# A four-stage token kernel on one Trainium2 core: the modulation row spread by DMA instead of by matmuls, the output accumulated by halves, the attention penalties gathered by type

## The reference, cut to what matters

```
# layer 0, per sequence: 16 decaying sums over time of the same gated input
gated  = x * sigmoid([x, ema(x)] @ Wg + bg)
mod    = 0.5 + sigmoid(gelu(x @ Wn1 + bn1) @ Wn2 + bn2)        # (256 tokens, 16)
traces = [causal_ema(gated * mod[:, d:d+1], tau_raws[d]) for d in range(16)]
temporal = sum_d traces[d] * softmax(blend)[d]
out = layernorm((gelu(x @ Wsoma) * sigmoid(temporal @ Wtemp)) @ Wout)
# layer 1, attention pooling: the score depends on the key alone, the mask on the type 0, 1 or 2
score[j, l] = v . tanh(W1 x[l] + b1)  -1e30 where l > j (type 0), l < j (type 1) or l == j (type 2)
# layer 2: 8 experts and a shared one, F = 1024, each scaled by a gate of the sequence
x += sum_e coef[e] * (silu(x @ Wg[e]) * (x @ Wu[e])) @ Wd[e]
# layer 3: a head with 192 shared output columns and 64 that are chosen per sequence
x += gelu(x @ W1 + b1) @ [W2, We[index]] + bias
```

## Time and profile before

| | |
|---|---|
| Runs shown | 2933.64, 2936.31 and 2940.9 us; median 2936.31 us |
| Profiled execution | 2936.55 us, of which the span from first to last instruction is 2934.7 us |
| Mean granted clock of PE | 0.986 of 2.4 GHz |
| Busy | PE 97%, PEld 81%, DVE 62%, ACT 49%, POOL 41% |
| Chain that ended last | PE 88%, DVE 7%, issue 2%, ACT 2% |
| DMA | 185.87 MB, on average 63 GB/s; share of the 16 engines' span 20% |

### The profile page before, as it was taken

How to read it: one execution, slowest core, us unless ns; L and a number is a source line. 1 busy time by engine, 2 the same in 40 slices (tenths; PEclk the granted TensorE clock), 3 DMA queues, 4 the chain that set the end, 5 groups by cost and what they waited for, 6 DMA issues and landing times.

```text
span 2934.7 us, 37380 instructions
## 1 busy us (share of the span) xinstructions
PE 2837.9 (97%) x13486; PEld 2373.1 (81%) x13486; DVE 1809.2 (62%) x2922; ACT 1433.5 (49%) x2466; POOL 1195.4 (41%) x931
## 2 busy tenths in 40 slices
PE   4799999999999999999999999999999999999998
PEld 3588888878888887887888888888888888888887
DVE  7669777776665586656665567566555556333443
ACT  1244663475345563456434555356533446334544
POOL 4216336524543345423454235532444433333333
PEclk7899999999999999999999999999999999999999
DMA  2222231121111121113111112111211112111331
GB/s 102 84 94 91 81 101 59 55 74 58 51 49 47 45 83 61 45 40 99 44 44 44 47 41 89 44 44 57 70 49 49 49 49 91 57 43 49 119 97 38
DMA packets 75688, 185.87 MB, mean 63 GB/s; under 512 B 8936, under 2 KB 21744, under 8 KB 75504
## 3 DMA queue, kind: packets, MB, share of 16 engines
q1 hardware_dynamic: 73648, 179.17, 19.5%
q0 software_dynamic: 1280, 4.20, 0.5%
q10 hardware_dynamic: 576, 0.11, 0.0%
HBM read 179.25 MB, written 4.19 MB: 63 GB/s over the span
## 4 chain that ended last, share of the span: by engine, by line
PE 88%; DVE 7%; issue 2%; ACT 2%; DMA 0%; POOL 0%; DVEq 0%; SPq 0%; ACTq 0%
PE bank L512 19%; PE bank L514 19%; PE bank L513 19%; PE ps_out L512 9%; PE ps_out L514 9%; PE ps_out L513 9%; PE bank L505 3%; DVE w_lo L1080 2%; DVE trace L994 2%; DVE trace L1002 1%; PE bank L582 1%; PE ps_out L667 1%; DVE hid L1109 0%; DVE acc L1126 0%; DVE trace L1060 0%
## 5 line engine op out<-in xcount | busy, mean ns | idle before, releaser
L1233 POOL TENSOR_TENSOR hid_lo<-hid,hid_hi 128x512 fp32r<-128x512 f32 (+1 forms) x640 | 849.1, 1327 | 1559.2 <-ACT hid_hi L886 1559.0
L512 PE MATMUL bank<-res_lo,w_hi 128*128 128x512 f32 (+1 forms) x2432 | 948.9, 390 | 4.7 <-issue 3.9
L514 PE MATMUL bank<-res_hi,w_hi 128*128 128x512 f32 (+1 forms) x2432 | 937.7, 386 | 0.0
L513 PE MATMUL bank<-res_hi,w_lo 128*128 128x512 f32 (+1 forms) x2432 | 936.9, 385 | 0.0
L1109 DVE TENSOR_TENSOR hid<-hid,bank 128x512 f32<-128x512 f32 (+1 forms) x608 | 399.1, 656 | 636.2 <-PE bank L514 526.5
L876 ACT ACTIVATE hid<-bank 128x512 f32<-128x512 f32 (+1 forms) x608 | 349.7, 575 | 728.5 <-PE bank L514 652.9
L1080 DVE TENSOR_TENSOR w_lo<-w_raw,w_hi 128x768 fp32r<-128x768 f32 (+1 forms) x488 | 441.7, 906 | 182.6 <-ACT w_hi L839 141.1
L514 PEld LDWEIGHTS bank<-res_hi,w_hi 128*128 128x128 f32 x2432 | 457.8, 188 | 96.8
L512 PEld LDWEIGHTS bank<-res_lo,w_hi 128*128 128x128 f32 x2432 | 458.0, 188 | 92.7 <-issue 5.7
L513 PEld LDWEIGHTS bank<-res_hi,w_lo 128*128 128x128 f32 x2432 | 458.5, 189 | 81.6
L839 ACT ACTIVATE w_hi<-w_raw 128x768 fp32r<-128x768 f32 x360 | 304.3, 845 | 443.9 <-PE ps_out L514 437.9
(11 more groups left out here) (178 smaller groups left out, 1948.6 us busy)
## 6 DMA issues: line engine op xcount, KB each, us to landing
w_raw<-in_chunks SPq DMA_DIRECT2D x360, 384.0 KB, 3.0
w_raw<-in_head_chunks SPq DMA_DIRECT2D x64, 224.0 KB, 2.4
plain<-in_chunks SPq DMA_DIRECT2D x32, 384.0 KB, 3.4
x_in<-in_xT SPq DMA_DIRECT2D x16, 256.0 KB, 3.4
out_yT<-acc SPq DMA_DIRECT2D x8, 512.0 KB, 2.8
acc<-in_sidew SPq DMA_DIRECT2D x2, 512.0 KB, 7.4
acc<-in_sidew SPq DMA_DIRECT2D x1, 320.0 KB, 5.8
mask<-in_masks SPq DMA_DIRECT2D x1, 256.0 KB
```

What stands on the lines that cost most here:

```text
L512: mm(out, wh, xl, start=start and i == 0, stop=False, skip_group_check=not lone)
L513: mm(out, wl, xh, start=False, stop=False, skip_group_check=not lone)
L514: last = mm(out, wh, xh, start=False, stop=end, skip_group_check=not lone)
L1233: nc.gpsimd.tensor_tensor(hid_lo[i % DEPTH][:, tok], hid[i % 3][:, tok], f(hid_hi[i % DEPTH][:, tok]), ALU.subtract).then_inc(s_hlo, 1)
```

## The change

- The mix of every lane but the lead is no longer a matmul. When DVE has scaled the modulation, SP writes its 16 rows to DRAM (`mod_rows`, piece 6). A new piece READ (number 47, between 6 and 7) reads them back with the same source for all 128 partitions: four DMAs of two rows each into `one_hi`, `one_lo`, `two_hi` and `two_lo`, which lie idle then, and four more, one in each of the pieces 9, 11, 13 and 15. DVE's product reads the row from SBUF. READ and piece 7 are in `ON_PE`, pieces 8 to 22 no longer are.
- Piece 5 does not split the modulation, outside the lead.
- The penalties come from a table of 3 x 128 rows in DRAM, of which POOL gathers 128 rows of 2 KB per sequence by an indirect DMA in a new piece (j = 24); piece 39 is then one addition.
- DVE adds `ps_out` into `acc` by channel halves: half 0 starts when PE has ended half 0 (`s_half`), and PE's next product into half 0 waits for that half only (`s_acc0`).

```diff
+READ = 47
+PIECE_ORDER = list(range(7)) + [READ] + list(range(7, PIECES))
-ON_PE = {2, 3, 4, 5, 27, 31, 33, 38, 39, 41, 44, 46} | set(range(7, 7 + ND))
+ON_PE = {2, 3, 4, 5, READ, 7, 27, 31, 33, 38, 39, 41, 44, 46}
...
+        mod_on = [[f(t[s][:]) for t in (one_hi, one_lo, two_hi, two_lo)] for s in range(BB)]
+        mod_rows = nc.dram_tensor("mod_rows", (B, ND * S), fp32, kind="Internal").ap()
...
+            def modulation(b, s, j):
+                q = b * BB + s
+                if j == 6:
+                    sp.wait_ge(l_dve[s], dve_at(s, b, "mod"))
+                    sp.dma_start(mod_rows[q].rearrange("(d t) -> d t", d=ND), stat[s][0:ND, :]).then_inc(s_mod[s], 16)
+                elif j == READ:
+                    sp.wait_ge(s_mod[s], 16 * filled(b, s))
+                    if b:
+                        sp.wait_ge(l_pe[s], pe_at(s, b, "gate"))
+                    for i in range(4):
+                        spread(q, s, i)
+                elif j in (9, 11, 13, 15):
+                    sp.wait_ge(l_dve[s], dve_at(s, b, f"mul{j - 8}"))
+                    spread(q, s, (j - 1) // 2)
+            def spread(q, s, i):
+                sp.dma_start(mod_on[s][i % 4].rearrange("p h t -> p (h t)"),
+                             mod_rows[q, 2 * i * S:2 * (i + 1) * S].partition_broadcast(P)).then_inc(s_on[s][i % 4], 16)
...
-                elif 7 <= j < 7 + ND:
+                elif 7 <= j < 7 + ND and lead:
...
-                    dve.wait_ge(l_pe[s], pe_at(s, b, f"mix{d}"))
+                    if lead:
+                        dve.wait_ge(l_pe[s], pe_at(s, b, f"mix{d}"))
+                    else:
+                        i = d // 2
+                        dve.wait_ge(s_on[s][i % 4], 16 * (2 * filled(b, s) - (i < 4)))
                     for h in range(DH):
                         last = STT(tr[:, h, :], gated[s][:, h, :], bl[:, h, d:d + 1],
-                                   (lead_mix[d % 2] if lead else ps)[:, 0:S], ALU.mult, ALU.mult)
+                                   lead_mix[d % 2][:, 0:S] if lead else mod_on[s][i % 4][:, d % 2, :], ALU.mult, ALU.mult)
...
-                    STT(score[:], mask[:, 0], pen[:, 0, q:q + 1],
-                        ps[:, 0:S].unsqueeze(1).broadcast_to([P, 2, S]), ALU.mult, ALU.add).then_inc(l_dve[s], 1)
-                    mine("sc0")
-                    STT(score[:], mask[:, 1], pen[:, 1, q:q + 1], score[:], ALU.mult, ALU.add).then_inc(l_dve[s], 1)
-                    mine("sc1")
-                    for jh in range(2):
-                        diagonal = score[:, jh, jh * P:(jh + 1) * P]
-                        last = STT(diagonal, idn[:], pen[:, 2, q:q + 1], diagonal, ALU.mult, ALU.add)
-                    last.then_inc(l_dve[s], 1)
+                    TT(score[:], trace[s][2][:], ps[:, 0:S].unsqueeze(1).broadcast_to([P, 2, S]),
+                       ALU.add).then_inc(l_dve[s], 1)
...
+                for h in range(DH):
+                    if h == 0:
+                        dve.wait_ge(s_half, CLOSES[i])
+                    else:
+                        dve.wait_ge(s_down, i + 1)
...
+                                last = STT(X[:, h, tok], ps_out[:, h, tok], coef[:, e, q:q + 1],
+                                           lone_x[:, h, :] if i == FC - 1 else X[:, h, tok], ALU.mult, ALU.add)
+                    if h == 0:
+                        last.then_inc(s_acc0, 1)
...
+                if j == 24:
...
+                    pool.wait_ge(l_pool[s], pool_at(s, b, f"add{ND - 1}"))
+                    q = b * BB + s
+                    nc.gpsimd.indirect_dma_start(
+                        out=trace[s][2][:].rearrange("p j l -> p (j l)"), out_offset=None, in_=penalties[:],
+                        in_offset=bass.IndirectOffsetOnAxis(ap=pen_row[:, q:q + 1], axis=0)).then_inc(s_pen[s], 16)
```

More of the change, by code:

```diff
@@ L121, in order @@
         for _ in range(fill.get(j, 0)):
-            out.append(("side", 0, 1, ahead))
+            out.append(("side", 0, 1, PIECE_ORDER[ahead]))
             ahead += 1
     rest = []
-    lanes = [[(b, s, j) for b in range(NBLK) for j in range(PIECES)] for s in range(BB)]
+    lanes = [[(b, s, j) for b in range(NBLK) for j in PIECE_ORDER] for s in range(BB)]
     had = [0.0, LAG]
-    for s, n in ((0, PIECES), (1, ahead)):
+    for s, n in ((0, len(PIECE_ORDER)), (1, ahead)):
         had[s] += sum(side_cost(b, j) for b, _, j in lanes[s][:n])
@@ L253 @@
 SPLITS = {"x_hi", "ctx_hi", "t_hi", "p_hi", "q_hi", "x_lo", "ctx_lo", "t_lo", "p_lo", "q_lo", "xT_lo", "probT_lo"}
+FIRST_ONLY = {"mod_hi", "modpair"} | {f"mix{d}" for d in range(ND)}
 def at(stages, s, b, name):
-    plain = [x for x in stages if x not in SPLITS]
+    plain = [x for x in stages if x not in SPLITS and (s == 0 or x not in FIRST_ONLY)]
+    stages = [x for x in stages if x not in FIRST_ONLY]
     if s == 0 and "soma" in plain:
@@ L315, in residual_stack_kernel @@
         small = [sb(f"small{s}", [P, S]) for s in range(BB)]
-        mod_pair = [sb(f"mod_pair{s}", [P, S], f32r) for s in range(BB)]
+        mod_pair = sb("mod_pair", [P, S], f32r)
         stat = [sb(f"stat{s}", [P, S]) for s in range(BB)]
@@ L391, in residual_stack_kernel @@
         s_we = [sem(f"we_in{i}") for i in range(2 * BB)]
+        s_pen = [sem(f"penalty_in{s}") for s in range(BB)]
+        s_mod = [sem(f"mod_out{s}") for s in range(BB)]
+        s_on = [[sem(f"mod_in{s}_{i}") for i in range(4)] for s in range(BB)]
         s_y = [sem(f"y_out{i}") for i in range(NACC)]
@@ L481, in _ @@
                 fetch(n)
+            def modulation(b, s, j):
[15 more added lines that the diff above has]
+                             mod_rows[q, 2 * i * S:2 * (i + 1) * S].partition_broadcast(P)).then_inc(s_on[s][i % 4], 16)
             for x in ORDER:
+                if x[0] == "side" and (x[1] or x[2]):
+                    modulation(*x[1:])
                 if x[0] == "side" and x[3] == 0 and x[1] + 1 < NBLK:
@@ L668, in back_plain @@
                               start=c == 0, stop=c == FC - 1)
+                    if h == 0 and c == FC - 1:
+                        last.then_inc(s_half, 1)
                 last.then_inc(s_down, 1)
@@ L1118, in back @@
                     done("lo0")
-                dve.wait_ge(s_down, i + 1)
                 if last_close.get(b):
@@ L1283 @@
     key = np.arange(S)
-    masks = np.stack([key > j[:, :, None], key < j[:, :, None]], 1).reshape(P, -1).astype(np.uint16) * 0x3F80
+    allowed = np.stack([key <= j[:, :, None], key >= j[:, :, None], key != j[:, :, None]])
+    penalties = np.where(allowed, 0.0, NEG).astype(f32).reshape(3 * P, -1)
     picks = np.zeros((P, ND), f32)
```

103 lines of the change are left out of this document (54 added, 49 removed).

## The result

The changed kernel takes 2946.28 us (median of 7 runs, 2940.82 to 2949.39), the kernel before 2934.54 beside it. The ratio is 1.0034, with a 95% interval of 1.0025 to 1.0044: slower by a third of a per cent, where 2897 us, 1.3% less, had been forecast. The profiled execution spans 2944.4 us.

A forecast was written before the change was run, and what follows sets the result against it. After the lead, PE's issue bounds the kernel, plus some waits of PE on DVE. 28 + 4 + 9 + 10 - 4 - 5 - 3 = 39 us off 2936.55 gave 2897 us, range 2871 to 2922.

The forecast's parts named there:

- Operands in SBUF: DVE's 480 products with both operands in SBUF: 0.31 us more each, 3 us lost, between 0 and 21.
- The second rival: DVE and POOL collide at products and traces' additions; waits of 1.5 us per lane reach PE: 2925 us, chance 0.17.
- The prediction's own mark for that rival: Mean time of DVE's products L1041: near 0.5 us if the forecast holds, 0.7 or more if DVE and POOL collide.
- the 4.7 us that PE had in hand: Slack at the next `hid` product: ended at 1337.6, PE needed it only at 1342.26, so late DVE loses nothing there.
- The mixes leave PE: On PE: 233 mixes after 90 us at 0.12 us win 28.0 us; their ended waits win 9, between 0 and 12.3.
- The lead: Before the first step: 2.5 us from mixes gone before the `Wout` product, 1.5 from penalties, together 4 us won.
- Halves and the score chain: PE's waits for the accumulation and for `prob` (11.9 + 6.8 us) shrink: 10 us won, between 0 and 18.7.
- The gathers: POOL's one more indirect DMA per sequence: 0.35 us for each of 14, 5 us lost, between 0 and 17.
- penalties + 1.5 in the lead: In the lead, penalties taking 2.2 us become one addition of 0.68, so 1.5 us go, counted within the lead's 4.
- counted at nothing: DVE time freed by the penalties, some 24 us, and by unsplit modulation, 15, lies beside PE's work: no gain taken.
- The reads: Modulation read through DRAM: first read 2.2 us late, 0.3 us for each of 14 lanes, 4 us lost, between 0 and 31.
- The third rival: Reads come late, the first landing after 11.3 us: 2980 us, middle of the case 2950, chance 0.10; turning at about 9 us.

The follow-up runs named there:

- row from PSUM: Changed kernel, product reading the side PSUM bank (a wrong factor) in place of the SBUF row, transfers and waits kept: 2896.47 us, ratio 0.9873.
- the addition moved: Changed kernel, POOL's addition of a trace waiting for the next product of its sequence instead of the scan, nothing left out: 2896.53 us, ratio 0.9872.
- the row in SBUF: Kernel before with mixes and waits kept, product reading the block's input in SBUF (a wrong factor) instead of the mix in PSUM: 2976.11 us, ratio 1.0143.
- modulation alone: Changed kernel with accumulation by halves and gathered penalties undone, leaving the modulation through DRAM and its order: 2963.00 us, ratio 1.0107.
- the remedies: Changed kernel with POOL's addition after the next product and the first half of the gated input in PSUM: 2891.67 us; without halves 2894.46.
- halves alone: Kernel before with only the accumulation by halves: 2935.40 us, ratio 0.9998.
- penalties alone: Kernel before with only the mask and its four instructions replaced by the gather and one addition: 2923.99 us, ratio 0.9958.
- the kernel whose DVE had become short: Changed kernel with penalties made from masks again, 2961.27 us, ratio 1.0083, set against the changed kernel with gathered penalties, 2946.28 us.

## Why the prediction was wrong, step by step

**The step that failed: "Operands in SBUF".** It read the right pair of rows, named the right partner, and then took 3 us, bounds 0 to 21. Measured: 50 us (row from PSUM; the added operand in the kernel before, 42). Three things in it were wrong.

*How often they meet, and what a meeting costs.* I took the stretch of L972, 0.31 us, as what any product would suffer, whatever stands beside it. Counted from the trace of the changed kernel, by what POOL does while a product runs:

```
beside POOL's            products of 480   mean us    with the addition moved: products, mean us
an addition                    284           1.12          12   0.67
only hid_lo                     43           0.81         152   0.87
neither                        153           0.475        316   0.474
```

An addition is released by the scan in front of the next product, so the two tend to start together: 284 meetings where chance, at POOL's 42% busy, would give fewer. A product that meets one more than doubles on average. It isn't slowed evenly but held: 271 products take over 0.6 us, and each of them ends 0.28 to 0.29 us after an instruction of POOL has ended, an addition or a `hid_lo`; the other 209 take at most 0.573. The trace of the kernel before has the meetings already: 298 of its 512 products run beside an addition, and with a PSUM operand none takes over 0.483 us. So their number could have been counted there. The second rival said just this ("just when the next lane's product comes"), and kept the price of the chance meeting. The prediction's own mark for that rival, a mean of 0.7 us or more, was passed: 0.884.

*How much of it reaches PE.* "At most 150 us are added to DVE [...] inside the 995 us that DVE is not busy" is an average, and the 4.7 us that PE had in hand come from one step. The row from PSUM takes 199 us off DVE, more than those 150, and 50 off the run; the row in SBUF put 144 on DVE and 42 on the run. So a quarter or more of what DVE gains or loses at the products arrives at PE. I took 2% (3 of 150). The bound, 1.5 us for each of 14 sequences, was an estimate of a wait at one place per sequence; there are 16 pairs of products in each. The loss came early, where DVE is fullest (78% busy from 235 to 660 us before, 81% after). Start times of three of the 4162 matmuls into `ps_out`, the same ones in each kernel:

```
matmul      before    changed    modulation alone    row from PSUM    addition moved
59           164.5     -12.1          -11.2             -17.7           -20.2
767          655.0     +16.9          +24.2             -18.2           -16.8
4071        2896.2     +10.0          +20.5             -38.2           -38.5
```

The numbers behind the first column are differences from it. The changed kernel is 12 us ahead at matmul 59 and 17 behind at matmul 767. From there on it wins some of that back, at a slower rate than the kernel with the row from PSUM.

*What a wait of PE costs.* I priced a wait at its length. Behind PE's longest one, 5.56 us for the accumulation, ending at 1792.07, the windows show:

```profile
1780.00:1786.00 6.00, 6.00 (x28) 4.99 (x27) 5.93 (x11) 4.75 (x14) 4.17 (x3) 1.00 0.17 64
1786.00:1792.00 6.00, 0.51 (x3) 0.09 (x1) 5.96 (x17) 1.94 (x3) 0.60 (x1) 0.89 0.57 176
1792.00:1798.00 6.00, 5.93 (x18) 5.00 (x19) 6.00 (x5) 1.28 (x2) 5.67 (x5) 0.55 0.66 218
1798.00:1804.00 6.00, 6.00 (x36) 5.20 (x35) 5.97 (x7) 4.52 (x8) 3.79 (x4) 1.00 0.32 98
```

The granted clock is 0.55 in the 6 us after the wait, so mostly the lower level of 1.2 GHz, and PE starts 18 matmuls there, in the next 6 us at full clock 36. At this place about half of the wait's price is paid a second time, an estimate from the 18 and 36. Matmuls over 0.6 us after 235 us, as those of 512 columns are at the lower clock: 21 before, 68 in the changed kernel, 25 with the addition moved, but also 45 with the row from PSUM, which is as fast. They count as busy, which is part of why PE's busy time fell by 18 us only. How much of the 50 us the clock makes was not tried.

The Trainium skill ("SBUF — State Buffer", Who interferes with whom) has the rule that I cited and priced low: a DVE instruction with two SBUF inputs contends with GpSimd's reads, and the one that issues later fully blocks. The trace agrees: 0.475 us alone and 1.12 on average beside an addition of 1.3 to 1.5 us, with the 271 ends of products right behind an end on POOL. Its summary of rules says to schedule the one off the critical path; here that is the addition, and moving it is what worked.

**The mixes leave PE: 28 + 9.** The first term held. With the row from PSUM, PE's busy time is 31 us below that of before, where 28.8 were to be expected of 240 mixes. Net of the reads the removal is worth 22 us (2918.8 to 2896.5); with some 10 us for the reads, an estimate from the kernel without them, about 32 of the 37. L617 has 16 matmuls left, as said.

**The lead: 4.** The product into `Wout` starts at 57.38 (62.14 before), the transposes of `prob` at 77.97 (83.81): 4.8 and 5.8 us. Right, a little small.

**Halves and the score chain: 10.** Halves gave 0 alone, 5 us beside the gathered penalties (2924.0 to 2918.8), 3 with the remedies. The waits for the accumulation shrink as worked out (11.9 to 7.9 us with halves alone), and nothing shows of it in the end. In the changed kernel they grew to 18.8. Even with the row from PSUM they are 12.9, and those for `prob` 6.1 (6.8 before; 7.4 with the penalties alone), so these waits did not close where DVE had its time back either.

**The gathers: -5, penalties + 1.5 in the lead, 24 us of DVE "counted at nothing".** Wrong in sign. Penalties alone won 11 us, 15 in the kernel whose DVE had become short (2961.3 to 2946.3). Sixteen gathers at 1.17 us of POOL are there; what they cost is below what they save. The row that gave them their price, DVE's L1060 pair of 3.21 us, was misread. The first of the pair takes 2.95 us (0.35 where nothing stands beside it) and ends 0.16 us after the second `hid_lo` of POOL has ended, 2.68 us after the gather. So most of the price was that of `hid_lo`: the instruction was held until POOL's had ended, as the products are, though it has only one tensor operand. In the changed kernel five products ran beside a gather for the head alone and took 0.48 us. Of the DVE time that I had called covered, about half came back as time. Which of the effects (lead, score chain, freed DVE, the changed pace) gave how much was not tried.

**The reads: -4, bounds 0 to 31.** Mechanism right, size small. DVE waits at the first trace only: 22.6 us in 9 times, the longest 3.7, with a landing of 3.4 us as taken from the earlier trace rows. Leaving them out gives 10 us. Later reads never made DVE wait. The third rival, a read landing after 9 us, did not occur: the longest was 7.3. The write to DRAM was bounded too low: 2.8 us by the earlier trace rows, measured 3.8 in the median and 7.3 at the longest. The Trainium skill ("DMA: Bandwidth & Descriptors", Anatomy of one DMA), from which the prediction has its 2.6 us, gives that fit for DMAs that GpSimd issues; these are issued by SP, and the first of the four reads landed after 3.4 us in the median.

**The sum.** 28 + 4 + 9 + 10 - 4 - 5 - 3 missed by 49 us. The operand alone is 47 of that (50 for 3); the reads are 6 more, halves with the score chain and mixes give some 5 less each, and the penalties, 11 us won for 3.5 lost, take 15 off again: 47 + 6 + 5 + 5 - 15 = 48. That the kernel with its row from PSUM came to 2896.5, where the sum without its operand term gives 2894.5, is partly luck, since the penalties' error covers the others.

## What to carry to other kernels

An operand moved from PSUM to SBUF is not free even where the transfer that brings it is hidden: look at what POOL runs at that instant, above all at what this very instruction's chain releases on POOL, since such meetings come from the order of the work and not from chance (284 of 480 here, and countable in the trace of the kernel before). Microseconds added to an engine that isn't the bound aren't covered by its average idle time; find what fraction reaches the bound engine by adding a known amount (here a quarter or a little more). And when two engines collide, first try to move the start of the one with time in hand behind an instruction that doesn't collide: one changed wait was worth 50 us.

## What the runs showed of the hardware beyond what I expected

- A single column that is broadcast along the free axis as a tensor operand counts as a full second SBUF operand: the scan takes 1.074 us with its decay in SBUF, 0.676 with it in PSUM. The column `bl`, the product's scalar operand, does not: with it and the gated input in SBUF and the row in PSUM the product takes 0.475 us beside an addition too.
- After a wait of PE of 5.56 us the granted clock is 0.55 over 6 us, and half as many matmuls are started in them.
- Around a pair of gathers one pair of products took far more than one addition explains (DVE, then POOL, of the changed kernel):

```profile
1793.48 4.97 DVE L1041 SCALAR_TENSOR_TENSOR trace<-gated,bl,two_lo 128x256 f32<-128x256 f32 x2
...
1792.67 1.72 POOL L1266 DMA_INDIRECT we_in<-in_we_rows,ex_row  x1 [0.30 <-issue]
1794.41 2.52 POOL L1291 TENSOR_TENSOR hid_lo<-hid,hid_hi 128x512 fp32r<-128x512 f32 x2
1796.89 1.27 POOL L1285 TENSOR_TENSOR temporal<-temporal,trace 128x512 f32<-128x512 f32 x1
```

POOL's three instructions behind the gather run back to back until 1798.16, and DVE's next one, the scan, starts at 1798.48 (0.87 us is what such a pair takes alone). The first product of the pair takes 0.48 us. The second runs from 1793.88 to 1798.45, so it was held for all three of them and not for one. Whether the gather, which ends at 1794.38, took part isn't told by this.
